# Deformable sampling in an eight-image fp32 block: four gather patches instead of two, index words a pair ahead, tap rows in strips, and the weighting done by small operations on two engines

## The reference

```python
xn  = gn(x)                                   # group norm, 32 groups of 8 channels
off = conv3x3(xn, offset_w) + offset_b        # 2 offsets for each of 4 groups
mod = 1 + tanh(conv3x3(xn, mod_w) + mod_b)    # 1 factor for each of 4 groups
v   = conv1x1(xn, kv_w[256:]) + kv_b[256:]    # 8 heads x 32 channels
s   = bilinear(v, pixel position + off) * mod # per pixel and group: 4 corners, 4 weights
x1  = x + conv1x1(s, out_w) + out_b
x2  = x1 + zca(gn(x1)) * weight + bias        # whitening over 16 groups of 16 channels
```

## Time and profile before

| | |
|---|---|
| median of 3 runs | 6903.72 us (6898.48 to 6908.78) |
| profiled execution: span | 7542.0 us; no time beside the span is given for it |
| mean granted clock of TensorE | 0.806 |
| busy: TensorE matmul, VectorE, ScalarE, GpSimd | 4572.0, 4223.0, 1067.2, 4578.9 us |
| first and last gather of GpSimd | 289.6 and 6805.8 us |

### The profile page before, as it was taken

The page is one execution under the profiler, slowest core; times in us unless marked ns, Lnnn a source line. Parts: engine busy times, 40 slices in busy tenths (PEclk is TensorE's granted clock), DMA queues, the critical chain, the costliest instruction groups (busy, mean ns, idle before and its releaser), DMA issues.

```text
span 7542.0 us, 73500 instructions
## 1 busy us (share of the span) xinstructions
PE 4572.0 (61%) x17916; PEld 2935.6 (39%) x17916; DVE 4223.0 (56%) x8110; ACT 1067.2 (14%) x2723; POOL 4578.9 (61%) x4115
## 2 busy tenths in 40 slices
PE   5765656565566656655665656566665544446777
PEld 3443434344344433333443434343443333234322
DVE  6655656555565555555655556555555544345555
ACT  1211111111111111111111111111111111010000
POOL 0377667676767767667676677676776777770000
PEclk9877778787788878777887878787887766667999
DMA  8866657666666666666666666565565544445999
GB/s 283 275 203 212 200 185 227 195 205 201 197 206 207 209 194 208 197 193 207 202 216 196 201 206 217 188 216 186 184 195 183 187 131 136 129 129 193 421 421 412
DMA packets 1069670, 1612.36 MB, mean 214 GB/s; under 512 B 92080, under 2 KB 617008, under 8 KB 1067568
## 3 DMA queue, kind: packets, MB, share of 16 engines
q0 software_dynamic: 196608, 537.13, 22.2%
q10 hardware_dynamic: 632832, 536.91, 22.0%
q1 hardware_dynamic: 240176, 537.77, 20.7%
HBM read 1074.58 MB, written 536.87 MB: 214 GB/s over the span
## 4 chain that ended last, share of the span: by engine, by line
another core or an unknown queue 21%; issue 21%; PE 19%; DVE 18%; DMA 9%; POOL 5%; DVEq 3%; ACT 3%; ACTq 1%; POOLq 0%; SPq 0%
PE psA L929 6%; DVE patch L568 5%; PE psO L965 5%; POOL patch L829 5%; DMA out_dram<-vring 4%; DVE patch L570 4%; PE psG L994 3%; DMA vring<-x 3%; PE psT L954 2%; DVE xr L582 2%; DMA v<-vring 1%; DVE vring L483 1%; PE psT L979 1%; DVE bst L418 1%
## 5 line engine op out<-in xcount | busy, mean ns | idle before, releaser
L829 POOL DMA_INDIRECT patch<-v,index_now x4096 | 4572.9, 1116 | 2224.0 <-issue 1517.0
L568 DVE TENSOR_TENSOR patch<-patch,weight 128x2048 f32<-128x2048 f32 x512 | 1171.3, 2288 | 941.4 <-DMA patch<-v,index_now 553.1
L929 PE MATMUL psA<-wB,xa 128*128 128x364 f32 x3824 | 1498.5, 529 | 185.2 <-DVE taps L486 103.1
L979 PE MATMUL psT<-ident,xr 128*128 128x128 f32 x2048 | 373.8, 343 | 1712.3 <-issue 928.5
L582 DVE SCALAR_TENSOR_TENSOR xr<-psO,bo_sb,xr 128x512 f32<-128x512 f32 x512 | 375.2, 748 | 1205.9 <-remote 972.5
L979 PEld LDWEIGHTS psT<-ident,xr 128*128 128x128 f32 x2048 | 300.6, 177 | 1917.7 <-issue 1067.8
L965 PE MATMUL psO<-sampT,wO_sb 128*128 128x512 f32 x2048 | 985.3, 626 | 73.4 <-issue 42.1
L929 PEld LDWEIGHTS psA<-wB,xa 128*128 128x128 f32 x3824 | 769.6, 218 | 574.4 <-issue 208.8
L954 PE MATMUL psT<-ident,samp 128*128 128x128 f32 x2048 | 409.9, 329 | 674.2 <-DVE samp L573 440.1
L1126 ACT ACTIVATE x1T<-psT 128x512 f32<-128x512 f32 x512 | 290.0, 596 | 3629.8 <-PE psT L979 1597.1
L994 PE MATMUL psG<-x1T 128*128 128x129 f32 x4096 | 664.6, 329 | 29.8 <-issue 18.7
(11 more groups left out here) (176 smaller groups left out, 2935.5 us busy)
## 6 DMA issues: line engine op xcount, KB each, us to landing
v<-vring ACTq DMA_DIRECT2D x256, 1024.0 KB
xa<-x_dram SPq DMA_DIRECT2D x256, 512.0 KB
xr<-x_dram SPq DMA_DIRECT2D x256, 512.0 KB
x<-xr ACTq DMA_DIRECT2D x256, 512.0 KB
xs<-x_dram SPq DMA_DIRECT2D x224, 512.0 KB
taps<-x SPq DMA_DIRECT2D x96, 1024.0 KB, 13.4
out_dram<-taps ACTq DMA_DIRECT2D x96, 1024.0 KB, 18.9
patch<-v,index_now POOLq DMA_INDIRECT x4096
```

What stands on the lines that cost most here:

```text
L568: eng.tensor_tensor(v4, v4, w4, ALU.mult).then_inc(weighted, 1)
L829: eng.indirect_dma_start(out=patch[j][:, t, :], out_offset=None, in_=v2_flat[k], in_offset=bass.IndirectOffsetOnAxis(ap=index_now[j][:, t: ...
L929: mm = eng.matmul(conv_bank[wide][r][:, 0:NA], xa[j][:, c, r * W:(r + 1) * W], wB[:, c, :], start=(c == 0), stop=(c == CC - 1))
L979: mm = eng.transpose(psT[h][:, at:at + P], xr[j][:, c, row * W:(row + 1) * W], ident[:, :])
```

## The change

Five parts:

1. `patch` and `index_now` become rings of four (n = 2 * (pair parity) + j), so a gather may run up to four blocks deep, and waits for the sample of the same block two pairs earlier. The pair loop is unrolled by two.
2. `indices` moves to the head of ScalarE's block. It now copies the weights too (64 numbers, `weight_now`) and serves the next pair.
3. ScalarE multiplies corners 0 and 2 of each row and group by their weights, in `scale`: 16 operations of 128 x 64 for each half block, with the weight as a per-partition scale operand.
4. VectorE's first two operations of a half become 16 `scalar_tensor_tensor` of 128 x 64 (odd corner x weight + even corner); the last addition stays.
5. `taps` becomes two strips of ten rows; the rows at a strip's edge are written twice. `y_buf` moves to patch 2 and 3 and to the memory of xa and xs. In the convolution-only pass TensorE's `offsets` moves ahead of row 3.

```diff
+RING = 4
+SAMP_FREE = 4
-        taps = sb("taps", [P, H + 2, NT])
+        taps = sb("taps", [P, 2, QR + 2, NT])
-        patch = [sb(f"patch{j}", [P, NJ, PATCH]) for j in range(2)]
+        weight_now = [sb(f"weight_now{n}", [P, NJ * 4]) for n in range(RING)]
+        patch = [sb(f"patch{n}", [P, NJ, PATCH]) for n in range(RING)]
...
-            pair(0)
-            with eng.Fori(1, PAIRS - 1) as i:
-                pair(i)
-            pair(PAIRS - 1)
+            pair(0, 0, 0)
+            with eng.Fori(0, PAIRS // 2 - 1) as h:
+                pair(eng.snap(h * 2 + 1), 1, h)
+                pair(eng.snap(h * 2 + 2), 0, eng.snap(h + 1))
+            pair(PAIRS - 1, 1, PAIRS // 2 - 1)
...
+                    if row == 0 and top:
+                        eng.memset(taps[:, 1 - m, QR + 1, :], 0.0)
+                        eng.memset(taps[:, m, 0, :], 0.0)
+                    elif row == 0:
+                        eng.tensor_tensor(taps[:, 1 - m, QR + 1, :], bank[:, C:NA], biasB[:, C:NA],
+                                          ALU.add)
+                    elif row == QR - 1:
+                        eng.tensor_tensor(taps[:, 1 - m, 0, :], bank[:, C:NA], biasB[:, C:NA],
+                                          ALU.add)
+                    eng.tensor_tensor(taps[:, m, row + 1, :], bank[:, C:NA], biasB[:, C:NA], ALU.add)\
...
+            def sample(b, i, m, j, h):
+
+                n = 2 * m + j
+                half = (b * PAIRS + i) * 4 + 2 * j + h + 1
+                eng.wait_ge(scaled, half)
+                for t in range(h * NH, (h + 1) * NH):
+                    for k in (0, 2):
+                        even = patch[n][:, t, k * CG:(k + 1) * CG]
+                        odd = patch[n][:, t, (k + 1) * CG:(k + 2) * CG]
+                        last = eng.scalar_tensor_tensor(
+                            even, odd, weight_now[n][:, t * 4 + k + 1:t * 4 + k + 2], even,
+                            ALU.mult, ALU.add)
+                last.then_inc(weighted, 1)
+                eng.wait_ge(weighted, half)
+                if h == 0:
+                    eng.wait_ge(psT_free[CC - 1], (b * PAIRS + i) * 4 + 2 * j + SAMP_FREE - 3)
+                mine = patch[n][:, h * NH:(h + 1) * NH, :]
                 eng.tensor_tensor(samp[j][:, 2 * h:2 * h + 2, :].rearrange("p r (g e) -> p (r g) e", g=G),
-                                  mine[:, :, 0:CG], mine[:, :, CG:ENT], ALU.add)\
+                                  mine[:, :, 0:CG], mine[:, :, 2 * CG:3 * CG], ALU.add)\
                    .then_inc(sampled[j][h], 1)
...
+            def scale(b, i, m, q, j, h):
+
+                n = 2 * m + j
+                eng.wait_ge(index_cp, (b * PAIRS + i) * 2 + j + 1)
+                eng.wait_ge(got[n][h], (b * (PAIRS // 2) + q) * (NH * 16) + NH * 16)
+                for t in range(h * NH, (h + 1) * NH):
+                    for k in (0, 2):
+                        corner = patch[n][:, t, k * CG:(k + 1) * CG]
+                        last = eng.activation(corner, corner, ACT.Copy,
+                                              scale=weight_now[n][:, t * 4 + k:t * 4 + k + 1])
+                last.then_inc(scaled, 1)
...
                     for j in range(2):
+                        if not last:
+                            if g is not None:
+                                indices(g, i + 1, 1 - m, j)
+                        elif a is not None:
+                            indices(a, 0, 0, j)
                         if g is not None:
+                            scale(g, i, m, q, j, 0)
                             if j == 1:
                                 x1_store(g, i, 0)
                                 x1_out(g, i, 0)
...
                         if g is not None:
+                            scale(g, i, m, q, j, 1)
                             samples_out(g, i, j)
-                        if not last:
-                            if g is not None:
-                                indices(g, i + 1, j)
-                        elif a is not None:
-                            indices(a, 0, j)
```

More of the change, by code:

```diff
@@ L134, in deform_zca_kernel @@
         gram_tail = sb("gram_tail", [P, B, CC, P + 1])
-        xs = [sb(f"xs{j}", [P, CC, BP]) for j in range(2)]
+        xs_mem = sb("xs_mem", [P, 2, CC, BP])
         bst = sb("bst", [P, CC, BLOCKS, 6])
@@ L469, in prep, with conv_out @@
                 eng.wait_ge(psI_free, b * NU + 3)
-            def conv_out(b, i, j, rows, wide):
+            def conv_out(b, i, m, j, rows, wide):
+                top = ends(i)[0]
                 for r in rows:
-                    k = r % 2
+                    k, row = r % 2, j * ROWS + r
                     eng.wait_ge(row_full[j][r], b * PAIRS + i + 2)
@@ L610, in pair @@
                     prepare = last and ca is not None
+                    if last and a is not None and s is None:
+                        eng.memset(taps[:, m, QR + 1, :], 0.0).then_inc(edge, 1)
                     for j in range(2):
                         if g is not None:
-                            sample(g, i, j, 0)
+                            sample(g, i, m, j, 0)
                             if j == 1:
@@ L647, in first_conv @@
                 for j in range(2):
-                    conv_out(0, 0, j, range(ROWS), True)
+                    conv_out(0, 0, 0, j, range(ROWS), True)
             run(eng, image, first_conv)
@@ L839, in _ @@
                     alone(eng)
-                    with eng.Fori(0, PAIRS) as i:
-                        for j in range(2):
-                            gather(b, k, i, j)
+                    with eng.Fori(0, PAIRS // 2) as q:
+                        for m in range(2):
+                            for j in range(2):
+                                gather(b, k, q * 2 + m, m, j)
         def whiten_tensor(eng):
@@ L931, in conv_rows, with offsets @@
                     mm.then_inc(row_full[j][r], 1)
-            def offsets(b, q, more):
+            def offsets(b, q, m, more):
+                bottom = ends(q)[1] and not more
                 for k in range(2):
-                    eng.wait_ge(psA_free[k], (b * PAIRS + q) * 4 + 5 + (0 if ends(q)[1] else 2))
+                    eng.wait_ge(psA_free[k], (b * PAIRS + q) * 4 + (5 if bottom else 7))
+                if bottom:
+                    eng.wait_ge(edge, 1)
                 eng.wait_ge(psI_free, offsets_use(b, q, more))
@@ L1021, in pair @@
                                 prep(ca)
-                            conv(range(ROWS))
-                            if j == 1:
-                                offsets(a, i, s is not None)
+                            if j == 0:
+                                conv(range(ROWS))
+                            else:
+                                conv((0, 1, 2))
+                                offsets(a, i, m, s is not None)
+                                conv((3,))
                         elif prepare and j == 0:
```

97 lines of the change are left out of this document (47 added, 50 removed).

## The result

The changed kernel takes 7202.56 us (median of 4, 7200.97 to 7215.95) against 6901.1 us of the kernel before (median of 4): ratio 1.0441 [1.0428, 1.0454], 4.4% slower.

A forecast was written before the change was run, and what follows sets the result against it. GpSimd bounds the kernel before at 22.7 us a block; afterwards the ScalarE-VectorE loop does at 24.3 (21.65 in the last image): 6136 us, plus 74 and 1026 outside, makes 7236 us; range 6590 to 7560.

The forecast's parts named there:

- GpSimd is freed by small operations: Small operations instead of L568 no longer hold off GpSimd's gathers: up to 684 us freed, 20.0 us a block.
- The row of hand-overs: ScalarE and VectorE hand each block back and forth four times without overlap: 23.8 us before Tanh and TensorE additions.
- ScalarE 0.23 us apart: Start distance of ScalarE's 64-column scale operations, the middle of bounds 0.15 and 0.31; sixteen take 3.82 us.
- TensorE's lower level: Transposes run slower at TensorE's lower clock level, about two fifths of the time: 0.4 us added to a block.
- The changes of image at 74 us: The 74 us of waits in the kernel before, kept as the cost of the seven changes of image.
- The ends: Time outside the gathers: 290 us ahead, 736 behind, 1026 in all; last image's 32 blocks at 21.65 us each.
- The sum: 224 x 24.3 + 32 x 21.65 = 6136 us, plus 74 and 1026: 7236 us; loop-bound range 7000 to 7500.
- The 74 us of waits before: All waits left in the median of the kernel before, beside 5804 us of gathers and 1026 us outside.
- Ring, index words, strips: Ring and early index words remove at most 74 us of waits, only while GpSimd bounds; strips put at nothing.
- the hand-overs are cheap: Rival: ScalarE's scales start 0.19 us apart or less, so the change gains: 6596 or even 6220 us; chance 0.28.
- GpSimd not freed: Rival: sixteen small operations hold gathers off like L568; GpSimd stays at 22.7 us a block, about 6900; chance 0.08.
- no overlap on VectorE: Rival: VectorE's small operations start 0.29 us apart, 1.2 us more each half, 26.7 a block, about 7770; chance 0.06.

The follow-up runs named there:

- the early scale: Changed kernel with ScalarE's scale of half 1 moved directly behind that of half 0: 6275.47 us, ratio 0.9088 on an undisturbed chip.
- the constant scale: Changed kernel with constant 0.5 instead of the weights of corners 0 and 2 as ScalarE's scale: 6466.43 us, ratio 0.937 on an undisturbed chip.
- the kernel with large operations: Changed kernel with VectorE's three large operations of before and no ScalarE scale; ring, early index words and strips stay: 6906.68 us, ratio 1.0005.

## Why the prediction was right

The forecast was 7236 us; measured 7202.56, 0.5% below. Point by point:

- *GpSimd is freed by small operations*: right. Of 4096 gathers 124 were stretched by the last addition L575 by over 0.1 us (41 us in all over the median of 946 ns), and 1282 that began beside L567 lost 21 us together, where L568 had cost 684 by the forecast's reckoning.
- *The row of hand-overs*: its pieces in the block shown, with the predicted value behind: samples written to scale 4.16 with the Tanh, 3.50 without (3.6, and 0.1 for the Tanh); scale 3.96 (3.82); VectorE's half 4.07 (4.17); to the second scale 4.11 (4.2); then 3.95 and 3.98 (3.82, 4.17). The means of 210 blocks (the first seven images, without the two blocks at each change) tell it better: 3.70 + 3.96 + 4.01 + 4.22 + 3.95 + 3.98 = 23.82 us, against 3.7 (the Tanh's 0.1 with it) + 3.82 + 4.17 + 4.2 + 3.82 + 4.17 = 23.88. No piece is off by more than 0.2 us. One piece begins where the last one ends, so their sum has to be the block; that a block gets shorter with a piece is what the early scale and the constant scale show. Within the first piece the Tanh is worth about 0.2 a block (3.92 us in the blocks behind it, 3.48 in the others), twice its term.
- *ScalarE 0.23 us apart*: sixteen took 3.92, so (3.92 - 0.336) / 15 = 0.239. With a constant, (2.44 - 0.243) / 15 = 0.146. The Trainium skill, "ScalarE: Activation LUTs", section "What ACT_TABLE_LOAD costs", has 93 ns for each pointer operand; the trace agrees, 336 less 243. From its formula the prediction worked out an estimate of 0.24 us between two starts; the trace has 0.239. Had I taken that price I would have written 7310, further off, since the next term was too large. So the middle of 0.15 and 0.31 was a guess that came near: no row had a scale operand.
- *TensorE's lower level, 0.4 us a block*: mis-sized, because it was added to a row that didn't need it. The lower level does lengthen the hand-overs: where the eight transposes of x1 took over 1.4 us instead of 1.07 (58 of the 210 blocks), the second one took 4.64 us instead of 4.07, which is 0.16 us a block. The transposes of the samples took 1.11 us, the slow value of the earlier trace rows, in 204 of the 210, and the copy L1125 began 0.72 us behind their start instead of 0.49. Yet the means above hold all this already and still are the sum without the term: the other parts of the hand-overs were that much shorter than reckoned. The mean block is 23.83 us instead of 24.3: 106 us less over 224.
- *The changes of image at 74 us*: mis-sized. The two blocks at a change take 66.4 us in the mean instead of 47.7, 131 us over seven (the last, ahead of the image without convolutions, takes 47.8; the other six 69.4). By the program, statistics, the new biases and four `conv_out` stand between two samples there, each waiting for the engine before it; which of them costs how much was not taken apart.
- *The ends*: 304.7 us ahead of the first gather instead of 290; 42.7 from it to the first sample and 31 blocks of 21.44 in the last image, 707 instead of 32 x 21.65 = 693; 734 behind the last sample, where the forecast had 736 behind the last gather.
- *The sum*: -106 + 57 + 15 + 14 - 2 = -22, and 7236 less 22 is the 7214.2 us of the span. Errors of opposite sign make the forecast look finer than its terms were: that it is within 0.5% is luck, that it is within the loop's range isn't.
- *The 74 us of waits before*: the kernel with large operations has none of them and the time of before. Its mean gather is 1129 ns instead of 1116 (53 us), its gap 0.305 instead of 0.30 (19 us), and 11 us more lie ahead. So the 74 us may as well have been stretching and rounding; the one trace of the kernel before has pauses in it and can't decide it. For the forecast it made no difference.
- *Ring, index words, strips*: 1.0005 for the three together; none was tried alone.
- *The rivals*: that the hand-overs are cheap needed a start distance of 0.19 or less; it is 0.239. GpSimd not freed and no overlap on VectorE (0.197 apart, not 0.29) fell by the rows above. The price of the latter was added up wrongly: it left the last image at 21.65 us a block; with 2.4 us more there too it is about 7850, not 7770.

## What to carry to other kernels

When work is moved to a second engine, write down the row of hand-overs first: an engine that is busy for 43% can still add its whole share to every round, if its program puts the new work between two things that others wait for. The place in the queue was worth 927 us here, more than the whole change cost, and one moved line turned 4.4% slower into 9.1% faster. And look at the kernel before on a chip before believing a ratio: the early scale was 9% faster on a chip where the kernel before took 6901 us and 9% slower on three where it took 7440 to 7589.

## What was unexpected of the hardware

*A gather has one gate.* In the version with large operations 392 gathers had begun over 0.1 us before an L568 started and were still in flight: all lasted 0.94 to 0.97 us. 502 began over 0.1 us behind its start: they ended 0.82 us after L568's end, whatever their start. In the timeline above L568 ends at 3211.10 and the gather at 3211.93. So, by these rows, a gather needs VectorE out of the way only at one point, some 0.13 us into its 0.95 (0.95 less the 0.82 that remain). The same holds for L575 in the changed kernel: it ends at 3226.75, the gather beside it at 3227.56. It would explain the small operations, where a gather need wait no longer than for the next of their ends: 26 gathers of 1282 were stretched by over 0.1 us, none by more than 0.16 (with the second scale early 121 of 1242, 34 us in all, the longest by 0.36, more than one operation's 0.28, so there the explanation doesn't hold as it stands). The Trainium skill, "SBUF — State Buffer", section "Who interferes with whom", says that a VectorE instruction with two SBUF inputs contends with GpSimd's reads; the trace agrees for L568 and L575. That the length of one instruction sets the price, and not the sum of their lengths, is what these rows add.

*Pauses on some chips.* On three chips the kernel before took 7440 to 7589 us instead of 6901 and the changed kernel, on one of them, 8542 instead of 7203. The losses: 540 to 690 us for the kernel before, 578 with the large operations, 1340 for the changed kernel, 1650 to 1690 with the constant scale, 1820 to 1960 with the early scale. They aren't in proportion to the hand-overs between ScalarE and VectorE: the last three kernels have the same number of them, and the version without weighting, which has none for the scales, is still 6.4% slower than the kernel before there. The pauses show between the end of one engine's work and the start of the next, up to 4 us in the block above, and between instructions of one engine that wait for nothing, and on VectorE, with the scales on ScalarE, they fall nearly all into second halves. The cause stays open.
